# Two SBUF adds moved from accumulating transfers to GpSimd, the last tile in three pieces, and new instruction orders in an attention and expert-mix kernel

## What is computed

```python
q1 = fake_quant(layernorm(x)); q2 = fake_quant(ctx)      # 2x512x1024, 2x1024x1024
x = x + q1 @ q2                                          # attention part
xn = layernorm(x)
top2 = top_k(xn @ gate_w.T, 2)                           # 8 experts, softmax of two
res = xn @ base_w.T + base_b                             # 1024x1024 weights
low = xn @ lora_A.T                                      # 8 experts x rank 16
x = x + res + 2.0 * mix(low, lora_B, top2)
```

## Time and profile before

| what | value |
|---|---|
| median of 3 runs | 171.46 us |
| the profiled execution's own time | 171.14 us |
| its span, first to last instruction | 168.9 us |
| mean granted TensorE clock | 0.999 |
| TensorE busy | 94% of the span |
| VectorE busy | 71% |
| ScalarE busy | 54% |
| GpSimd busy | 11% |

### The profile page before, as it was taken

One profiled execution on the slowest core, in us unless ns is written; L12 is line 12 of the kernel. 1 busy time (PEld: TensorE's weight loads), 2 busy tenths in 40 slices (PEclk: granted clock), 3 DMA queues, 4 the chain that ended last, 5 costly groups with the idle time before them and its releaser, 6 DMA issues.

```text
span 168.9 us, 2344 instructions
## 1 busy us (share of the span) xinstructions
PE 159.1 (94%) x801; PEld 119.6 (71%) x801; DVE 119.2 (71%) x290; ACT 91.2 (54%) x140; POOL 18.4 (11%) x40
## 2 busy tenths in 40 slices
PE   5787999999699999999999999999999999999992
PEld 1243435698588888878888767877888888888881
DVE  4887899996699989998799777964388171540212
ACT  3479999758931556804547687437729536000000
POOL 3132222002003000002200230004004000000000
PEclk9999999999999999999999999999999999999999
DMA  4999999999999923303480999994994992300033
GB/s 106 389 417 409 411 408 377 272 339 387 287 349 297 194 95 66 124 0 63 92 157 20 154 192 161 284 247 75 208 157 82 177 276 87 120 8 0 2 124 124
DMA packets 22187, 32.69 MB, mean 193 GB/s; under 512 B 13856, under 2 KB 13856, under 8 KB 22176
## 3 DMA queue, kind: packets, MB, share of 16 engines
q1 hardware_dynamic: 20016, 25.20, 46.2%
q0 software_dynamic: 2016, 7.34, 23.8%
q10 hardware_dynamic: 144, 0.00, 0.0%
HBM read 22.05 MB, written 4.19 MB: 155 GB/s over the span
## 4 chain that ended last, share of the span: by engine, by line
PE 72%; DMA 18%; SPq 4%; ACT 2%; issue 1%; DVE 1%; ACTq 0%
PE ps_even L1051 26%; PE ps_odd L1051 21%; DMA w_raw<-in_w_t 13%; PE ps_att L996 8%; DMA ring<-in_ctx 5%; PE ps_g L1032 5%; PE ps_g L1035 2%; SPq L250 1%; PE ps_t L977 1%; PE ps_even L1094 1%; PE ps_odd L1094 1%; PE ps_even L1093 1%; PE ps_even L1092 1%; PE ps_odd L1093 1%; PE ps_odd L1092 1%
## 5 line engine op out<-in xcount | busy, mean ns | idle before, releaser
L1051 PE MATMUL ps_even<-w_hi,yt 128*128 128x512 f32 x128 | 38.0, 395 | 0.0
L1051 PE MATMUL ps_odd<-w_hi,yt 128*128 128x512 f32 x128 | 37.4, 403 | 0.0
L1051 PEld LDWEIGHTS ps_odd<-w_hi,yt 128*128 128x128 f32 x128 | 24.0, 188 | 5.9 <-issue 0.2
L996 PE MATMUL ps_att<-c,c1t 128*128 128x512 f16 x96 | 27.4, 382 | 0.3 <-DVE c L705 0.3
L1051 PEld LDWEIGHTS ps_even<-w_hi,yt 128*128 128x128 f32 x128 | 23.4, 188 | 4.8
L1032 PE MATMUL ps_g<-ag,yt 128*128 128x272 f32 x64 | 20.8, 364 | 1.6 <-DVE yt L743 1.6
L1051 PE MATMUL ps_even<-w_lo,yt 128*128 128x512 f32 x64 | 20.6, 392 | 0.0
L1051 PE MATMUL ps_odd<-w_lo,yt 128*128 128x512 f32 x64 | 19.9, 394 | 0.0
L1032 PEld LDWEIGHTS ps_g<-ag,yt 128*128 128x128 f32 x64 | 12.1, 189 | 4.6 <-issue 2.0
L435 ACT ACTIVATE qc<-ring,q_in,q_rec 128x1024 uint16<-128x1024 f32 x11 | 13.4, 1234 | 2.1 <-DVE c L705 1.4
L1051 PEld LDWEIGHTS ps_even<-w_lo,yt 128*128 128x128 f32 x64 | 11.9, 188 | 2.6
(11 more groups left out here) (112 smaller groups left out, 257.6 us busy)
## 6 DMA issues: line engine op xcount, KB each, us to landing
ring<-in_ctx SPq DMA_DIRECT2D x12, 512.0 KB, 9.5
w_raw<-in_w_t SPq DMA_DIRECT2D x8, 512.0 KB, 16.1
x_sb<-in_base_b POOLq DMA_DIRECT2D x8, 512.0 KB, 7.7
out_x<-x_sb SPq DMA_DIRECT2D x16, 256.0 KB, 2.5
x_sb<-in_x SPq DMA_DIRECT2D x7, 512.0 KB, 8.6
x_sb<-zfix POOLq DMA_DIRECT2D x6, 512.0 KB, 6.6
x_sb<-in_ctx SPq DMA_DIRECT2D x4, 512.0 KB, 6.8
ag_raw<-in_ag_t SPq DMA_DIRECT2D x1, 544.0 KB, 14.1
```

The costliest lines, as they stand in the source:

```text
L996: ins = pe.matmul(att_bank(t)[h][:, :], c1t[:, t % 4, k, :], c2[:, k, h * HALF:(h + 1) * HALF], start=(k == 0), stop=(k == CT - 1))
L1051: pe.matmul(ffn_bank[t % 2][h][:, :], rows_of(part, t, k), w[:, k, h * HALF:(h + 1) * HALF], start=start, stop=False)
```

## The change

The column correction of tiles 2 and 3 becomes an addition on GpSimd, from SBUF to SBUF. The last tile is computed in three pieces, 512, 256 and 256 columns, the third in the attention bank. The orders of all five programs are new; below stand the parts of them that the text speaks of.

```diff
+        LAST = TILES - 1
+        last_piece = [(ps_even[0], 0, HALF), (ps_even[1], HALF, HALF // 2), (ps_att[0], HALF + HALF // 2, HALF // 2)]
...
+            def add_zfix_here(t):
+                pool.wait_ge(zfix_ready, 2 * (t // TPB) + 2)
+                pool.wait_ge(qx_ready[t], 1)
+                pool.tensor_tensor(x_sb[:, t, :], x_sb[:, t, :], zfix[:, :], ALU.add).then_inc(zfix_added[t], 16)
...
             square_constants()
             scale_context(2)
+            quant_constants()
             scale_context(5)
-            quant_constants()
-            add_zfix(2)
-            add_zfix(3)
+            add_zfix_here(2)
             add_bias(0)
+            add_zfix_here(3)
             add_bias(2)
             add_bias(1)
+            add_bias(3)
             add_zfix(4)
             add_zfix(5)
             add_zfix(7)
             add_zfix(6)
-            add_bias(3)
```

SyncE, from the start (`load_first(0)`, `load_first(1)` stand ahead):

```diff
+            load_x(1)
             load_context(0)
             load_context(1)
-            load_x(1)
-            load_context(2)
-            load_context(3)
             load_x(2)
-            for k in range(4, 7):
+            for k in range(2, 7):
                 load_context(k)
             load_x(3)
-            load_context(7)
+            for k in range(7, 11):
+                load_context(k)
+            load_w(0)
+            load_context(11)
+            load_w(1)
+            load_w(2)
+            load_ag()
+            load_w(3)
+            load_w(4)
             load_b()
-            load_ag()
-            for k in range(0, 5):
-                load_w(k)
-            load_context(8)
             for k in range(5, 8):
                 load_w(k)
-            load_context(9)
+            load_context(12)
+            load_context(13)
             load_x(4)
-            load_context(10)
-            load_context(11)
             load_x(5)
-            load_context(12)
+            load_context(14)
+            store(0, 0)
+            load_context(15)
+            transpose_c1(4)
```

ScalarE, from `scale_x(3)` to `split_y_hi(1, 1)`:

```diff
             scale_x(3)
-            split_w_hi(0)
+            scale_context(8)
             take_c1t(3)
             first_guess(1, 0)
-            split_w_hi(1)
-            split_w_hi(2)
+            for k in range(0, 3):
+                split_w_hi(k)
             split_y_hi(0, 0)
+            split_ag_hi()
+            split_y_hi(0, 1)
             split_w_hi(3)
-            split_y_hi(0, 1)
-            split_ag_hi()
             split_w_hi(4)
             first_guess(1, 1)
-            for k in range(5, 8):
-                split_w_hi(k)
+            split_w_hi(5)
+            split_w_hi(6)
+            split_y_hi(1, 0)
+            split_w_hi(7)
+            scale_context(9)
+            scale_context(10)
```

VectorE, the start and the stretch after the attention of tiles 0 and 1:

```diff
             variance(0, 0)
-            byte_ones(2)
+            variance(0, 1)
             x_constants(0)
             quantise_x(0)
...
             add_zfix(1)
+            split_w_lo(0)
             split_y_lo(0, 0)
             variance(1, 1)
+            split_ag_lo()
             split_y_lo(0, 1)
-            split_ag_lo()
             normalise_x1(1)
-            split_w_lo(0)
+            add_attention(2)
             split_w_lo(1)
+            split_w_lo(2)
+            split_y_lo(1, 0)
             top_logits(0)
-            add_attention(2)
-            split_y_lo(1, 0)
             variance(1, 2)
```

```diff
+            base_last(0, 0)
             transpose_low(7)
+            base_last(0, 1)
+            base_last(0, 2)
             lora(6, 0)
             lora(6, 1)
+            for k in range(3, 8):
+                base_last(0, k)
+            lora_last(0)
+            lora_last(1)
+            for k in range(3, 8):
+                base_last(2, k)
+            lora_last(2)
```

More of the change, by code:

```diff
@@ L578, in _ @@
-            first_guess(1, 2)
-            split_b_hi()
             exp_gate(1)
[L581 to L584, removed]
             split_y_hi(2, 0)
             split_low_hi(1)
+            first_guess(0, 4)
+            split_y_hi(2, 1)
+            scale_context(12)
             scale_x(4)
-            for k in range(11, 14):
-                scale_context(k)
-            split_y_hi(2, 1)
+            scale_context(13)
@@ L797, in split_low_lo, with finish_last @@
                 dve.tensor_tensor(lt_lo[:, :], low_t, lt_hi[:, :].bitcast(F32), ALU.subtract).then_inc(ltlo_ready, 1)
+            def finish_last(p):
+                bank, a, n = last_piece[p]
+                if p == 0:
+                    dve.wait_ge(bias_added[LAST], 16)
+                    dve.wait_ge(rowfix_ready, TILES)
+                    dve.wait_ge(ffn_half, TILES)
+                elif p == 1:
+                    dve.wait_ge(ffn_third, 1)
+                else:
+                    dve.wait_ge(ffn_done, TILES)
+                dve.scalar_tensor_tensor(out=x_sb[:, LAST, a:a + n], in0=bank[:, 0:n],
+                                         scalar=rowfix[:, LAST:LAST + 1], in1=x_sb[:, LAST, a:a + n],
+                                         op0=ALU.add, op1=ALU.add).then_inc(out_ready, 1)
             def finish_tile(t):
@@ L859, in _ @@
             split_low_lo(0)
+            weigh_low(1)
             variance(0, 4)
-            weigh_low(1)
+            split_y_lo(2, 0)
+            finish_tile(0)
+            cut_context(9)
             x_constants(4)
-            split_y_lo(2, 0)
-            split_low_lo(1)
[L865 to L872, removed]
+            cut_context(10)
+            cut_context(11)
+            add_attention(3)
+            cut_x(4)
+            sum_context(1)
+            split_y_lo(2, 1)
+            split_low_lo(1)
+            variance(1, 3)
             sum_context(2)
             cut_context(12)
+            normalise_x1(3)
             sum_context(3)
@@ L927, in _ @@
             finish_tile(4)
+            finish_tile(5)
             top_logits(6)
             weigh_low(6)
+            split_words_lo(7)
             split_low_lo(6)
-            split_words_lo(7)
-            finish_tile(5)
             top_logits(7)
@@ L936, in _ @@
             finish_tile(6)
-            finish_tile(7)
+            for k in range(0, 3):
+                finish_last(k)
         @block.tensor
@@ L1047, in bank_free, with one_pass @@
                         pe.wait_ge(zfix_ready, 4)
-            def one_pass(t, k, part, w, halves, start):
-                for h in halves:
+            def one_pass(t, k, part, w, start):
+                for h in range(2):
                     pe.matmul(ffn_bank[t % 2][h][:, :], rows_of(part, t, k), w[:, k, h * HALF:(h + 1) * HALF],
@@ L1232, in _ @@
             low_and_gate(3, 7)
-            for k in range(5, 8):
-                base(3, k)
+            lora(2, 0)
+            base(3, 5)
+            base(3, 6)
             lora(2, 1)
+            for k in range(0, 3):
+                attention(6, k)
             transpose_low(3)
-            for k in range(0, 4):
-                attention(6, k)
+            attention(6, 3)
+            attention(6, 4)
+            base(3, 7)
+            attention(6, 5)
+            attention(6, 6)
             lora(3, 0)
             lora(3, 1)
+            attention(6, 7)
             low_and_gate(4, 0)
-            attention(6, 4)
             low_and_gate(4, 1)
-            attention(6, 5)
-            low_and_gate(4, 2)
-            attention(6, 6)
-            low_and_gate(4, 3)
-            attention(6, 7)
             base(4, 0)
             base(4, 1)
+            low_and_gate(4, 2)
+            attention(7, 0)
+            low_and_gate(4, 3)
+            attention(7, 1)
             low_and_gate(4, 4)
-            attention(7, 0)
-            base(4, 2)
             low_and_gate(4, 5)
-            attention(7, 1)
+            attention(7, 2)
             low_and_gate(4, 6)
-            attention(7, 2)
+            attention(7, 3)
             low_and_gate(4, 7)
-            attention(7, 3)
-            for k in range(3, 6):
+            for k in range(2, 7):
                 base(4, k)
@@ L1263, in _ @@
             attention(7, 4)
-            base(4, 6)
             base(4, 7)
             low_and_gate(5, 0)
+            low_and_gate(5, 1)
             attention(7, 5)
-            low_and_gate(5, 1)
+            low_and_gate(5, 2)
             attention(7, 6)
-            low_and_gate(5, 2)
             low_and_gate(5, 3)
+            low_and_gate(5, 4)
             attention(7, 7)
-            for k in range(4, 8):
+            for k in range(5, 8):
                 low_and_gate(5, k)
-            for k in range(0, 3):
-                base(5, k)
+            base(5, 0)
+            base(5, 1)
             lora(4, 0)
+            base(5, 2)
             lora(4, 1)
```

340 lines of the change are left out of this document (178 added, 162 removed).

## The result

| | before | changed |
|---|---|---|
| median | 171.41 us (171.02 to 171.63) | 174.75 us (173.97 to 174.96) |
| ratio, 95% interval | | 1.0189 (1.0152 to 1.0227) |
| profiled execution: own time, span | 171.14, 168.9 us | 173.97, 171.8 us |
| TensorE busy | 159.1 us (94%) | 160.8 us (94%) |
| software queue's share | 23.8% | 20.2% |

The change makes the kernel slower by 3.3 us. The forecast was slower by 1.0, and its range ended at 173.3. The direction was right, and the size was not. The profiled execution is the fastest of the changed kernel's four, so its trace shows 2.8 us of the 3.3.

What follows compares the result with a forecast made beforehand. TensorE's work plus its gaps was taken as the bound (busy 94% of the span). Terms -1.6 - 0.4 + 1.7 + 0.7 + 0.3 + 0.3 + 0 = +1.0 on 171.46 gave 172.5 us, range 169.9 to 173.3.

Steps and rivals of the forecast that it cites:

- the second addition: GpSimd's addition for tile 3, behind `add_bias(0)`, holds VectorE at about 38 to 40 us: +0.3, bounds 0 and 1.2.
- The first addition: GpSimd's addition for tile 2, from about 24.0 us, holds VectorE's own addition to tile 0: +1.7, bounds 0 and 2.6.
- No blocking: Rival, chance 0.34: GpSimd and VectorE add side by side, or VectorE starts first; 170.5 us, faster.
- The stall: TensorE's wait of 1.62 us at 42.8 us for `split_y_lo(1, 0)` goes: -1.6.
- The first 30 us: Start of the kernel: attention slices moved ahead fill TensorE's gaps of 0.8 and 0.3: -0.4, bounds 0 and -0.9.
- `split_w_lo(0)`: On VectorE ahead of `split_y_lo(0, 0)`, it delays TensorE's first base product: +0.7, bounds 0.2 and 1.2.
- The tight places between 53 and 77 us: Steps there arrive within 0.3 us of TensorE's need: +0.3, bounds 0 and 0.9.
- The replay: Going through the new order with the old durations, used to find TensorE's gaps and tight places.
- The last tile: End of kernel: smaller last eviction -0.3 and store -0.1, against 0.4 for splitting 512-column matmuls: 0 in sum.
- Weights late: Rival, chance 0.08: weight slices land late behind contexts without GpSimd blocking, TensorE waits for high parts: 172.1 us.

Runs made afterwards that it cites:

- experiment 9: Changed kernel, first GpSimd addition after VectorE's `add_zfix(0)`, second released by the first half of `add_attention(2)`, ahead of `add_bias(0)`: 172.26 us, ratio 1.0032.
- experiment 1: Changed kernel, GpSimd's first addition (tile 2) waits until VectorE's `add_zfix(0)` is done: 171.56 us, ratio 1.0018.
- experiment 6: Kernel before with only the two additions of tiles 2 and 3 moved to GpSimd, other orders and last tile as before: 172.28 us, ratio 1.007.
- experiment 3: Changed kernel, GpSimd's first addition waits for VectorE's `add_zfix(0)`, its second for `split_w_lo(2)`: 171.12 us, ratio 0.9989.
- experiment 10: Kernel of experiment 3 with `split_w_lo(0)` behind `split_y_lo(0, 0)`, as before the change: 171.46 us, ratio 1.0002.
- experiment 12: Kernel of experiment 3 with `base(3, 5)` moved ahead on TensorE and `join_y(4)` ahead of `split_low_hi(3)` on ScalarE: 170.02 us, ratio 0.9882.
- experiment 11: Kernel of experiment 3 with the last tile in two halves of 512 columns, as before the change: 171.83 us, ratio 1.0016.
- experiment 7: Changed kernel with accumulating transfers back in place of GpSimd's two additions, new orders and last tile kept: 173.13 us, ratio 1.0119.
- experiment 4: Kernel before plus a GpSimd addition of `zfix` to itself into an unused buffer, once `zfix` is there: 171.17 us, ratio 0.9966.
- experiment 5: Kernel before plus a GpSimd memset into an unused buffer, once `zfix` is there: 171.18 us over three executions, ratio 1.0042.
- experiment 8: The changed kernel measured and traced a second time, unedited: 175.51 us, ratio 1.02.

## Why the prediction was off

**The step that failed is the second addition, put at +0.3.** The text had it run "from about 38 to 40 us, where VectorE normalises tile 1 and splits weights", and reckoned with "up to 0.9" of holding. It ran from 40.09, and met the two weight splits, both with two inputs from SBUF. They were held for 2.0 in one trace and 2.7 in the other. Only 1.0 of that was slack (0.4 to 0.6 had been reckoned), so TensorE's gap was 0.97 and 1.71. The medians put the term at 2.0 in the presence of the first collision. Alone it is 1.1 in experiment 9, just under the upper bound of 1.2, and 0.4 in experiment 1. Of the 2.3 us that the sum lacks, 1.7 lie in this term; most of the rest is in the late waits named below. The rule of the first addition, applied fully to the second, would have given it: a hold is as long as what is left of GpSimd's instruction (up to 2.1 by the forecast's own estimate, less 0.5 of slack), wherever VectorE has a two-input instruction next. And the terms depend on each other: the first collision moves VectorE by 1.8 and GpSimd, which waits for a transfer, not at all. The forecast added them as if they were independent.

**The first addition, +1.7, was right.** The length came out at 3.08 where "3 us" was named, `transpose_y(0, 0)` at 32.09 behind a wait of 1.67 where 31.7 and 1.7 were named. The medians give 1.6. That GpSimd's read is the cause is shown by the memset beside the spare addition. The Trainium skill, page "SBUF — State Buffer", section "Who interferes with whom", has this rule, and adds that a GpSimd instruction that only writes does not contend with one of two SBUF inputs; the traces agree (1.23 beside the memset, 2.55 beside the addition). It also says that a VectorE `tensor_scalar` may enter a mode that takes both port pairs; the 2.15 for 0.81 of experiment 6 agrees. The rival *No blocking* fell with the first trace. Its sum without the two additions, 170.5, stands against 171.12 in experiment 3.

**The stall, -1.6,** was right: it is gone, because ScalarE takes the transposed y ahead of the last slice. That slice came 0.7 us earlier, though, and not 1.9: GpSimd's issue of `add_bias(0)`, which waits for it, is at 39.32 for 40.02, and in the second trace at 40.74. For the term nothing hung on it; for the second collision it sets when GpSimd comes. **The first 30 us, -0.4,** gave -0.1 in the first trace and, with its late start, +0.6 in the second. **`split_w_lo(0)`, +0.7,** shows as 0.75 at that place but isn't a cost of the order: experiment 10 undid it and the time stayed. **The tight places between 53 and 77 us, +0.3,** cost nothing, while two places named nowhere, at 91.6 and 107.6, cost 0.18 and 0.40, and with small ones 0.9 in all (the lag grows from 1.8 to 2.7); experiment 12 got 1.1 back there. The replay went no further than 77 us, and the new orders did. **The last tile, 0,** was right in both halves: 256-column matmuls start 0.12 apart (0.122 forecast; 27 x (0.240 - 0.228) = 0.3 for the split, 0.4 forecast), the eviction takes 0.48 (0.44), the tail is 0.4 shorter. In medians experiment 11 can't tell it from nothing.

*Weights late* had no part in the changed kernel: ScalarE took the slices without a wait. It shows a little in experiment 7, where the transfers are back: 0.2 for a high part. GpSimd's addition took 2.36 where 2.1 was estimated from the rows. The estimate of 2.25 from the Trainium skill, page "GPSIMD Engine Reference", section 3.1, was the nearer.

## What to carry to other kernels

Moving an elementwise step onto GpSimd is not free because GpSimd is idle: list what VectorE does in the window of GpSimd's instruction, and if it has an instruction there with two SBUF inputs (or a one-input one such as the normalisation of experiment 6, seen once), the later of the two waits for the rest of the earlier. Then place GpSimd's step with a wait, beside statistics or PSUM work; two such waits turned 174.75 us into 171.12. And where a transfer releases one of the engines, the winner can change from execution to execution, so one trace can understate or overstate the price.

## What the runs showed of the hardware

- A GpSimd addition of two 128x1024 float32 tiles takes 2.36 to 2.41 us alone (1.89 in experiment 4, where both inputs are the same tile), VectorE's 1.23. Held, the one is listed with up to 3.13 and the other with 3.08. A trace gives no wait for this: the time stands inside the instruction that is held, and TensorE's gap behind it is put down to "issue".
- Holding goes both ways, by who is first (experiments 1 and 6 show GpSimd held), and also with a one-input normalisation (0.81 to 2.15, once). That was not expected.
- GpSimd's one-input instruction on a tile took 1.19 both times in the changed kernel, with no VectorE cut starting beside it, and 1.45 and 1.40 before. So those rows, taken as lengths, probably held some contention; it was not tried by itself.
- Two accumulating transfers fewer bring the issue that waits for the last weight slice forward by 4.6 us with the old order of the loads (experiment 6: 35.45 for 40.02) and by 3.2 with the new one (experiment 3 against 7: 39.47 for 42.67), where 5.7 was reckoned. Against the kernel before, the changed one gained only 0.7, since three more contexts stand ahead of that slice.
- After a wait of 2.21 us TensorE went on at 2.4 GHz for 1.1 us, then ran at 1.2 GHz for 3.4 us (experiment 5). After waits of 1.62 and 1.71 us (kernel before, experiment 8) the granted clock stayed at 1.00.
